# Finer interleaving of finishing work with a first convolution, and a later place for the strip copies

## The chip, the cores and the metric

One Trainium2 chip, one NeuronCore of it. The metric is device time in microseconds (us) of one execution; the kernel before has a median of 6257.3 us over 3 runs (6242.81 to 6264.0). Engines: PE is TensorE (matmuls and transposes), DVE is VectorE, ACT is ScalarE, POOL is GpSimd, SP is SyncE, which here only issues DMAs.

## The reference

For each of 16 samples x of 128 x 160 x 160, all in float32:

```
xp   = einsum('bchw,oc->bohw', x, proj_w)          # 128 -> 64 channels
att1 = route(xp,   depthwise 3x3 or 5x5)           # one kernel chosen per sample, by argmax of pooled logits
att2 = route(att1, depthwise 7x7, 9x9 or 11x11, dilation 3)
out  = concat([att1, att2])                        # 128 channels
a    = [mean over channels, max over channels] of out
gate = sum of the 2 channels of sigmoid(conv7x7(a) + sp_b)
result = out * gate + x
```

## The kernel before, in words

The program works on samples in turns. `samples` unrolls turns 0 to 3 and 15 to 17 and loops over 4 to 14. In turn s four samples are in work at once (`Turn`): sample s is projected and goes through the first convolution; sample k = s-1 goes through the second convolution; sample m = s-2 gets its gate and the second half of its output; sample n = s-3 gets the rest of the first half. All engines have their own hand-written order of work and meet by semaphores.

PE's turn has three stages, one behind the other:

- **Projection** (L947, L956 turns the result round): six blocks of rows of x. Behind fill 8 stands `turn_map2(m)` (L968), which turns the channel sums and maxima of sample m. DVE spreads them (`spread2`, L1326), SP stores them to `map2_d` (`store_map2`: L427 loads the other half, L436 stores) and loads both back (`load_maps`, L442). DVE's `combine` (L1332) waits for that, and only behind it come the last block's sums, the routing's small steps, and so the choice of weights that the first convolution needs. The 7x7 convolution of the maps is `spatial` (L1021).
- **First convolution** of sample s, 32 pairs of channels (`conv1`, L1011 and L1012). ACT widens and doubles each pair's band of weights and copies the result out (L823, L829, L834). Between the pairs stand pieces of *finishing* work that share the two banks psB: `turn_gate` ("gt", L1029); ten *f1* pieces (u = 6 to 15) of sample n, each 10 transposes (`finish1`, L1053) behind a product on DVE (`gate1`, L1397) and followed by DVE's two additions (L1406); and the five *f2* units of sample m, each 9 steps of 3 transposes (`finish2`, L1042), each step followed by DVE's additions into a tile xf (L1383). DVE multiplies L by the gate, one product per unit (`gate2`, L1364). A table `AFTER` says behind which group of two pairs which piece stands.
- **Second convolution** of sample k (L1074), 16 groups of 4 channels. POOL doubles its weights (L671), ACT brings the input (L854) and takes the result (L864). Behind groups 11 to 15 stand six *early* f1 pieces (u = 0 to 5) of sample m.

What the queues do around it: SP's turn is the maps and the gate; the loads of xf; then for each f2 unit `store_xf` (L457), `land` (L475, four DMAs that bring a sixth of the strips of sample k into the part of L that the unit has freed) and `load_xf` (L449) for the unit after next, which needs the tile that the store empties. Then `store_att1` (L485, 24 DMAs to `nat_d`), the first loads of the early pieces (L492 and L499), the load of one block of x (L489), `make_strips` (L535, 18 DMAs from `nat_d` to `strip_d`, DRAM to DRAM), and `early_pieces`, which per piece issues a load of att1 (L492), a store (L505) and a load of x (L499). POOL loads the other blocks of x (L634) and serves the f1 pieces of sample n (L682, L689, L695). ACT's `bring` of the first group waits until all six lands of the turn are through.

Semaphore order that matters: an f2 step writes bank t % 2 and waits for the additions of step t-2; an f1 piece waits for all f2 additions so far, and f2 work behind an f1 piece waits for that piece's additions.

## Time and profile before

| what | value |
|---|---|
| median of 3 runs | 6257.3 us |
| the profiled execution | 6248.61 us, span 6246.9 us |
| busy PE / DVE / ACT / POOL | 78% / 50% / 45% / 16% |
| mean granted TensorE clock | 0.873 |
| DMA, mean over the span | 206 GB/s |

The span is the time from the first to the last instruction; 1.7 us lie around it. Busy shares overlap between engines. The granted clock is a share of full speed, 2.4 GHz; 0.50 is the lower level, 1.2 GHz. A DMA share of 1 means that the core's 16 DMA engines were busy throughout.

### The profile page before, as it was taken

To read this page: it belongs to the slowest core of one execution; us is meant where nothing else is said; L and a number is where in the kernel's file an instruction comes from. 1 tells how busy PE (TensorE), PEld (TensorE's weight loads), DVE (VectorE), ACT (ScalarE), POOL (GpSimd) and SP (SyncE) were. 2 spreads that over 40 slices of the span, in tenths; PEclk is the share of its full clock that TensorE was granted. 3 is DMA by queue.
4 is the path that set the end of the run, shared out by engine and by line. 5 is a ranking of instruction groups with operands and counts; after the bars stand their busy time and mean duration, and the time that the engine had idled before them with its cause. 6 is when DMAs were issued, how large, how long until landed. Compare 5 with 4: busy or idle time off the path is not lost.

```text
span 6246.9 us, 164652 instructions
## 1 busy us (share of the span) xinstructions
PE 4902.2 (78%) x62816; PEld 3305.9 (53%) x62816; DVE 3144.4 (50%) x3931; ACT 2831.7 (45%) x5378; POOL 1030.5 (16%) x1574
## 2 busy tenths in 40 slices
PE   5688888978888897888888887788888788785463
PEld 2236474645646465564646546464554646455352
DVE  3316356554545655464464546545454565545445
ACT  3465544544445454544545454454444445452120
POOL 2002011211112121111211111121111112111232
PEclk9899998988889998988989888898898889887675
DMA  9646677868788786878868687886869778687957
GB/s 230 204 116 211 163 217 196 219 199 221 220 213 228 194 215 200 222 229 210 228 186 216 202 214 219 214 228 180 225 206 228 221 199 220 197 209 185 220 136 194
DMA packets 1033287, 1285.69 MB, mean 206 GB/s; under 512 B 670749, under 2 KB 865736, under 8 KB 1001885
## 3 DMA queue, kind: packets, MB, share of 16 engines
q1 hardware_dynamic: 899468, 723.43, 47.9%
q0 software_dynamic: 64304, 410.01, 21.1%
q10 hardware_dynamic: 69026, 146.11, 8.6%
q8 instruction: 259, 4.24, 0.3%
q14 instruction: 230, 1.88, 0.1%
HBM read 950.16 MB, written 456.70 MB: 225 GB/s over the span
## 4 chain that ended last, share of the span: by engine, by line
PE 34%; DMA 23%; SPq 21%; issue 9%; DVE 8%; ACT 2%; ACTq 1%; POOL 1%; DVEq 0%; POOLq 0%
SPq L485 12%; PE psA L1011 9%; PE psA L1012 9%; DMA X<-nat_d 6%; DMA out_dram<-RX 6%; DMA RX<-in_x_dram 5%; PE psC L1074 4%; SPq L535 4%; PE psA L947 3%; PE psB L1042 3%; SPq L436 3%; PE psB L1021 2%; PE psB L1053 2%; DVE MM L1299 2%; PE psB L956 2%
## 5 line engine op out<-in xcount | busy, mean ns | idle before, releaser
L1074 PE MATMUL psC<-RX 61*60 61x120 f32 (+7 forms) x49152 | 1538.6, 273 | 327.9 <-issue 154.7
L1074 PEld LDWEIGHTS psC<-RX 61*60 61x60 f32 x49152 | 1462.0, 137 | 404.4 <-issue 398.3
L864 ACT ACTIVATE L<-psC 124x120 f32 (+4 forms) x2048 | 393.9, 284 | 1119.9 <-PE psC L1074 1084.6
L1011 PE MATMUL psA<-X,RX 128*128 128x240 f32 x1280 | 640.1, 589 | 126.0 <-ACT RX L829 125.0
L671 POOL COPY RX<-RX 64x720 f32<-64x720 f32 x512 | 416.4, 816 | 1828.5 <-DMA RX<-w_d 1825.2
L1042 PE MATMUL psB<-ident,L 124*128 124x124 f32 x2160 | 413.4, 334 | 323.8 <-DVE RX L1383 283.2
L834 ACT ACTIVATE X<-psA,bias 128x246 f32<-128x246 f32 x1024 | 636.9, 735 | 56.6 <-issue 30.5
L1299 DVE TENSOR_REDUCE MM<-L 124x135 f32<-124x2160 f32 (+1 forms) x192 | 535.3, 2843 | 243.9 <-ACT L L864 243.9
L1012 PE MATMUL psA<-X,RX 128*128 128x240 f32 x1280 | 632.4, 583 | 0.0
L1383 DVE TENSOR_TENSOR RX<-psB,RX 128x360 f32<-128x360 f32 (+7 forms) x1200 | 366.4, 352 | 475.2 <-DMA RX<-in_x_dram 247.3
L854 ACT ACTIVATE RX<-L 128x1080 f32 (+1 forms) x256 | 541.0, 2121 | 131.0 <-DMA L<-strip_d 131.0
L947 PE MATMUL psA<-RX,projt 128*64 128x512 f32 x1600 | 462.9, 662 | 138.5 <-DMA RX<-in_x_dram 50.1
L1275 DVE TENSOR_REDUCE MM<-X 128x246 f32<-128x15744 f32 x16 | 264.8, 16553 | 587.5 <-ACT X L834 587.5
L823 ACT ACTIVATE RX<-RX 32x640 f32<-32x640 f32 x320 | 234.1, 736 | 718.1 <-PE psA L1012 585.4
L1042 PEld LDWEIGHTS psB<-ident,L 124*128 124x128 f32 x2160 | 290.6, 172 | 471.3 <-issue 445.9
L787 ACT ACTIVATE RX<-psA 128x512 f32<-128x512 f32 x480 | 287.5, 599 | 443.8 <-PE psA L947 400.9
L956 PEld LDWEIGHTS psB<-ident,RX 128*128 128x128 f32 x1920 | 207.1, 144 | 455.1 <-ACT RX L787 268.0
L1011 PEld LDWEIGHTS psA<-X,RX 128*128 128x128 f32 x1280 | 267.0, 219 | 338.3 <-issue 314.8
L1397 DVE TENSOR_TENSOR X<-X,G 80x1280 f32<-80x1280 f32 x126 | 190.5, 1522 | 444.1 <-DMA X<-nat_d 434.9
L1012 PEld LDWEIGHTS psA<-X,RX 128*128 128x128 f32 x1280 | 284.0, 222 | 231.1 <-issue 212.7
L1011 PE MATMUL psA<-X,MM 128*128 128x240 f32 x768 | 383.7, 588 | 16.5 <-ACT MM L829 14.9
L1012 PE MATMUL psA<-X,MM 128*128 128x240 f32 x768 | 379.5, 583 | 0.0
(122 smaller groups left out, 4969.7 us busy)
## 6 DMA issues: line engine op xcount, KB each, us to landing
RX<-in_x_dram POOLq DMA_DIRECT2D x48, 2560.0 KB, 16.4
RX<-w_d ACTq DMA_DIRECT2D x512, 180.0 KB, 4.4
RX<-in_x_dram SPq DMA_DIRECT2D x128, 720.0 KB, 10.3
out_dram<-RX SPq DMA_DIRECT2D x128, 720.0 KB, 10.3
nat_d<-X SPq DMA_DIRECT2D x320, 280.0 KB
L<-strip_d SPq DMA_DIRECT2D x192, 405.0 KB, 12.4
strip_d<-nat_d SPq DMA_DIRECT2D x48, 1440.0 KB
RX<-nat_d POOLq DMA_DIRECT2D x130, 400.0 KB, 6.7
```

Source lines behind the costliest of these rows:

```text
L485: sp.dma_start(dst, X[32 * k:32 * k + n, b, t0:t0 + T1, :]).then_inc(att1_stored, 16)
L671: nc.gpsimd.tensor_copy(w2t[j][64:128, :, :], w2t[j][0:64, :, :]).then_inc(w2_doubled, 1)
L834: ins = nc.scalar.activation(X[:, :, :, c:c + 1].rearrange("p b t c -> p (b t c)"), psA[pair % 2][:, ch * N1:(ch + 1) * N1], ACT.Identity, ...
L854: nc.scalar.activation(binf[q].rearrange("p (c f n) -> p c f n", c=G, f=5), Lc[:, :, bass.ds(g * G, G)].rearrange("p (n f) c -> p c f n", ...
L864: ins = nc.scalar.activation(dst[:, 0:NU2 - par, 15 * r:15 * r + nq, par, :], src[:, par:BR:2, :, :], ACT.Identity)
L947: ins = nc.tensor.matmul(o, projt[:, :], xsb[b][:, :, w0:w0 + FW], start=True, stop=True)
L1011: nc.tensor.matmul(o[:, :, 0:T1], w[:, ch, 96:224], rhs, start=True, stop=False, skip_group_check=True)
L1012: ins = nc.tensor.matmul(o[:, :, 1:1 + T1], w[:, ch, 224:352], rhs, start=False, stop=True, skip_group_check=True)
L1042: ins = nc.tensor.transpose(psB[t % 2][:, 124 * f:124 * f + 124], L[0:124, slot * C2:slot * C2 + 128], ident[0:124, 0:124])
L1074: ins = nc.tensor.matmul(o[:, :, 0:kk, a:b], w2t[2 * q + p][rows, ch, z:z + PB], src[rows, 2 * p + ch, 0:nf, 3 * cg + dc:3 * cg + dc + kk, ...
L1299: nc.vector.tensor_reduce(dst[0:124, mm, :].rearrange("p (f b k) -> p f b k", f=9, k=3)[:, :, par:BR:2, :], src[:, :, 0:NU2 - par, :, par, ...
L1383: return nc.vector.tensor_tensor(d, view(psB[t % 2][rows, :], 64 * g0 + c0, sdims), d, ALU.add)
```

## The change

Three things are edited.

1. On SP, `make_strips(s)` is issued behind `early_pieces(m)` where it stood ahead of it.
2. The table is by pair of channels, no longer by group of two pairs, on PE and DVE. In turns with a first convolution the f1 pieces 6 to 15 stand behind pairs 0, 3, 6, ..., 27 and the gate's turn behind pair 3. (Before: behind pairs 1, 3, 7, 11, 15, 17, 19, 21, 23, 25 and 3.) Turn 17 has a table of its own, changed likewise.
3. The f2 work is cut into 23 chunks of two steps where it was five units of nine. They stand behind pairs 4 to 22, one a pair and two behind pairs 7, 11, 15 and 19. (Before: one unit behind each of pairs 5, 7, 9, 11 and 13.) A unit's gate product on DVE follows the ninth step of the unit two before it, now inside a chunk.

```diff
+STEPS2 = 9 * NU2
+AFTER = {pair: [] for pair in range(C2 // 2)}
+for _u, _pair in zip(range(EARLY, NU1), (0, 3, 6, 9, 12, 15, 18, 21, 24, 27)):
+    AFTER[_pair].append(("f1", _u))
+AFTER[3].insert(0, ("gt", 0))
+for _c in range((STEPS2 + 1) // 2):
+    AFTER[4 + _c - (_c + 1) // 5].append(("f2", _c))
...
                     if t.next:
                         load_x2(s + 1)
-                    make_strips(s)
                     if t.early:
                         early_pieces(m)
+                    make_strips(s)
...
-            def finish2(m, u):
-                wait_alone(pe, att2_gated, NU2 * m + u + 1)
-                for t9 in range(9):
-                    t = 9 * u + t9
+            def finish2(m, c):
+                for t in range(2 * c, min(2 * c + 2, STEPS2)):
+                    u, t9 = divmod(t, 9)
                     p, k = divmod(t9, 3)
+                    if t9 == 0:
+                        wait_alone(pe, att2_gated, NU2 * m + u + 1)
...
-                for g in range(NG):
+                for pair in range(C2 // 2):
                     if t.new:
-                        for pair in (2 * g, 2 * g + 1):
-                            conv1(s, pair)
-                    for what, u in t.after[g]:
+                        conv1(s, pair)
+                    for what, u in t.after[pair]:
                         if what == "f1" and t.one:
                             if t.two:
-                                wait_alone(pe, f2_add, 45 * m + 9 * halves)
+                                wait_alone(pe, f2_add, 45 * m + min(2 * halves, STEPS2))
...
                     ins.then_inc(f2_add, 1)
+                    if t9 == 8 and u < NU2 - 2:
+                        gate2(m, u + 2)
...
                                 finish2(m, u)
-                                if u < NU2 - 2:
-                                    gate2(m, u + 2)
```

How the order moves, at two places. On PE, turn 3, the first convolution: four matmuls of L1011 and L1012 are one pair of channels, L1042 (L1050 in the changed kernel) are the f2 transposes, L1053 (L1061) an f1 piece. Before:

```order
L1042 MATMUL psB<-ident,L 128x124 x27
L1011 MATMUL psA<-X,RX 128x6x40
L1012 MATMUL psA<-X,RX 128x6x40
L1011 MATMUL psA<-X,RX 128x6x40
L1012 MATMUL psA<-X,RX 128x6x40
L1011 MATMUL psA<-X,RX 128x6x40
L1012 MATMUL psA<-X,RX 128x6x40
L1011 MATMUL psA<-X,RX 128x6x40
L1012 MATMUL psA<-X,RX 128x6x40
L1042 MATMUL psB<-ident,L 128x124 x27
L1053 MATMUL psB<-ident,RX 128x80 x10
```

And now:

```order
L1050 MATMUL psB<-ident,L 128x124 x6
L1018 MATMUL psA<-X,RX 128x6x40
L1019 MATMUL psA<-X,RX 128x6x40
L1018 MATMUL psA<-X,RX 128x6x40
L1019 MATMUL psA<-X,RX 128x6x40
L1061 MATMUL psB<-ident,RX 128x80 x10
L1050 MATMUL psB<-ident,L 128x124 x6
L1018 MATMUL psA<-X,RX 128x6x40
L1019 MATMUL psA<-X,RX 128x6x40
L1018 MATMUL psA<-X,RX 128x6x40
L1019 MATMUL psA<-X,RX 128x6x40
L1050 MATMUL psB<-ident,L 128x124 x12
```

27 transposes in a row have become 6 behind each pair (12 behind every fourth), and an f1 piece now has f2 transposes directly behind it, which before had a pair of channels or more between.

On SP, turn 2, behind the first loads of the early pieces. Before, from the end of the strips (the last of their 18 rows):

```order
L535 DMA strip_d<-nat_d 5x960
L535 DMA strip_d<-nat_d 5x1600
L492 DMA X<-nat_d 80x2x640
L505 DMA out_dram<-X 64x800 x2
L492 DMA X<-nat_d 80x2x640
L505 DMA out_dram<-X 64x800 x2
L499 DMA X<-in_x_dram 64x800 x2
```

And now, from the load of x on, and from the last store:

```order
L496 DMA X<-in_x_dram 128x5120
L499 DMA X<-nat_d 80x2x640
L512 DMA out_dram<-X 64x800 x2
L499 DMA X<-nat_d 80x2x640
L512 DMA out_dram<-X 64x800 x2
```

```order
L512 DMA out_dram<-X 64x800 x4
L542 DMA strip_d<-nat_d 48x4x1920
L542 DMA strip_d<-nat_d 48x960
L542 DMA strip_d<-nat_d 48x1600
L542 DMA strip_d<-nat_d 6x4x1920
```

The 18 strip copies have gone from ahead of the third early load of att1 to behind the last early store, that is, to just ahead of the next turn's L427 and L436.

## Rows read from the trace of the kernel before

**Rows 1.** The page: the span; the chain that ended last, by line.

```profile
span 6246.9 us, 164652 instructions
...
SPq L485 12%; PE psA L1011 9%; PE psA L1012 9%; DMA X<-nat_d 6%; DMA out_dram<-RX 6%; DMA RX<-in_x_dram 5%; PE psC L1074 4%; SPq L535 4%; PE psA L947 3%; PE psB L1042 3%; SPq L436 3%; PE psB L1021 2%; PE psB L1053 2%; DVE MM L1299 2%; PE psB L956 2%
```

**Rows 2.** Windows: us, busy PE, PEld, DVE, ACT, POOL (instructions), clock, DMA share, GB/s.

```profile
2276.00:2400.50 124.50, 104.34 (x3113) 98.95 (x3114) 77.65 (x33) 53.09 (x139) 24.25 (x30) 0.87 0.89 256
2407.10:2481.80 74.70, 63.56 (x294) 27.23 (x294) 47.38 (x86) 39.69 (x68) 10.57 (x17) 0.91 0.46 145
2481.80:2644.30 162.50, 138.88 (x500) 81.12 (x501) 67.72 (x122) 83.63 (x127) 25.98 (x46) 0.90 0.88 213
482.20:587.60 105.40, 91.77 (x3074) 88.02 (x3076) 67.26 (x21) 52.95 (x139) 22.66 (x30) 0.95 0.82 247
```

**Rows 3.** Timeline of PE: start, us, what, [idle before, releaser]; first convolution, turn 7.

```profile
2481.83 1.14 PE L1011 MATMUL psA<-X,RX 128*128 128x240 f32 x2 [6.44 <-ACT RX L829]
...
2488.45 0.87 PE L1053 MATMUL psB<-ident,RX 80*128 80x80 f32 x10
...
2506.55 0.83 PE L1042 MATMUL psB<-ident,L 124*128 124x124 f32 x6 [0.42 <-DVE RX L1406]
...
2556.48 5.57 PE L1042 MATMUL psB<-ident,L 124*128 124x124 f32 x21 [8.16 <-DVE RX L1383]
```

**Rows 4.** Groups of instructions in that stage (xcount | busy us, mean ns | idle before).

```profile
L1042 PE MATMUL psB<-ident,L 124*128 124x124 f32 x135 | 24.7, 321 | 15.6 <-DVE RX L1383 14.6 <-DVE RX L1406 0.4
...
L1383 DVE TENSOR_TENSOR RX<-psB,RX 128x360 f32<-128x360 f32 (+7 forms) x75 | 22.8, 352 | 29.2 <-DMA RX<-in_x_dram 14.5 <-PE psB L1042 14.1
L1364 DVE TENSOR_TENSOR L<-L,G2s 124x3456 f32<-124x3456 f32 x5 | 18.7, 3751 | 0.0
```

**Rows 5.** Timeline of SP's issues in the same stage.

```profile
2526.06 12.59 SPq L475 DMA_DIRECT2D L<-strip_d  x4
2540.60 2.26 SPq L449 DMA_DIRECT2D RX<-in_x_dram  x2
...
2576.75 25.06 SPq L475 DMA_DIRECT2D L<-strip_d  x8
```

**Rows 6.** The page: DMA issues, KB each, us to landing.

```profile
L<-strip_d SPq DMA_DIRECT2D x192, 405.0 KB, 12.4
```

**Rows 7.** Timeline of PE in the second convolution of turn 6.

```profile
2354.12 4.27 PE L1074 MATMUL psC<-RX 61*60 61x135 f32 x96 [4.09 <-POOL RX L671]
...
2384.98 1.60 PE L1053 MATMUL psB<-ident,X 80*128 80x80 f32 x10 [4.54 <-DVE X L1406]
```

**Rows 8.** Timeline of SP's issues there, and in the projection behind it.

```profile
2341.19 19.12 SPq L535 DMA_DIRECT2D strip_d<-nat_d  x18
...
2402.96 6.05 SPq L505 DMA_DIRECT2D out_dram<-X  x4
...
2428.32 19.10 SPq L436 DMA_DIRECT2D map_d<-RX  x12
```

**Rows 9.** The chain of waits, in order of time, over the same stretch.

```profile
2360.67 22.14 DMA X<-nat_d
...
2389.02 4.17 DMA X<-nat_d
...
2453.60 3.71 DMA minc<-map_d
```

**Rows 10.** Windows of 20 us: the first two of the projection of turn 7.

```profile
2406.00:2426.00 20.00, 18.77 (x89) 7.69 (x89) 14.58 (x21) 11.18 (x19) 3.16 (x6) 0.85 0.14 36
2426.00:2446.00 20.00, 19.64 (x99) 7.55 (x100) 16.37 (x19) 12.92 (x23) 2.30 (x3) 1.00 0.79 283
```

**Rows 11.** Timeline of DVE: combine, in the same projection.

```profile
2457.33 0.83 DVE L1332 TENSOR_TENSOR minc<-RX,minc 48x640 f32<-48x640 f32 x1 [9.95 <-DMA minc<-map_d]
```

**Rows 12.** Timeline of PE in turn 16, which has no first convolution.

```profile
5839.99 1.47 PE L1042 MATMUL psB<-ident,L 124*128 124x124 f32 x6 [1.27 <-DVE X L1406]
...
5867.57 1.57 PE L1053 MATMUL psB<-ident,X 80*128 80x80 f32 x10 [11.23 <-DVE X L1406]
```

More of the change, by code:

```diff
@@ L61 @@
 EARLY = 6
-AFTER = {0: (("f1", 6),), 1: (("gt", 0), ("f1", 7)), 2: (("f2", 0),), 3: (("f2", 1), ("f1", 8)),
-         4: (("f2", 2),), 5: (("f2", 3), ("f1", 9)), 6: (("f2", 4),), 7: (("f1", 10),), 8: (("f1", 11),),
-         9: (("f1", 12),), 10: (("f1", 13),), 11: (("f1", 14),), 12: (("f1", 15),), 13: (), 14: (), 15: ()}
-AFTER_LAST = {0: (("gt", 0), ("f1", 0), ("f2", 0)), 1: (("f1", 1), ("f1", 2), ("f2", 1)), 2: (("f1", 3), ("f1", 4), ("f2", 2)),
-              3: (("f1", 5), ("f1", 6), ("f2", 3)), 4: (("f1", 7), ("f1", 8), ("f2", 4))}
-AFTER_LAST.update({g: (("f1", g + 4),) for g in range(5, 12)})
-AFTER_LAST.update({g: () for g in range(12, 16)})
+STEPS2 = 9 * NU2
[5 more added lines that the diff above has]
+    AFTER[4 + _c - (_c + 1) // 5].append(("f2", _c))
+AFTER_LAST = {pair: [] for pair in range(C2 // 2)}
+AFTER_LAST[0] = [("gt", 0), ("f1", 0)]
+for _c in range((STEPS2 + 1) // 2):
+    AFTER_LAST[1 + _c].append(("f2", _c))
+for _u in range(1, NU1):
+    AFTER_LAST[2 * _u].append(("f1", _u))
 def conv_block(nc, x, proj_w, w1, b1, w2, b2, att1_w, att1_b, att2_w, att2_b, sp_w, sp_b, out):
@@ L1365, in gate2, with finish2 @@
                                         ALU.mult).then_inc(att2_gated, 1)
-            def finish2(m, u):
-                q = u % 2
-                rows = slice(0, 128 if u < 4 else 64)
-                dve.wait_ge(xf_loaded[q], xf_count(m, u))
-                for t9 in range(9):
-                    t = 9 * u + t9
+            def finish2(m, c):
+                for t in range(2 * c, min(2 * c + 2, STEPS2)):
+                    u, t9 = divmod(t, 9)
+                    q = u % 2
+                    rows = slice(0, 128 if u < 4 else 64)
                     p, k = divmod(t9, 3)
+                    if t9 == 0:
+                        dve.wait_ge(xf_loaded[q], xf_count(m, u))
                     dve.wait_ge(f2_mm, 45 * m + t + 1)
@@ L1427, in turn @@
                         gate1(n, u)
-                for g in range(NG):
-                    for what, u in t.after[g]:
+                for pair in range(C2 // 2):
+                    for what, u in t.after[pair]:
                         if what == "f1" and t.one:
```

## The prediction

> **What bounds the kernel now.** I read the page first. No engine is full, and the chain that ended last changes hands all the time: SP's issues, transfers, PE [rows 1]. So the question is not how busy an engine is but what ends each stage of a turn. I therefore cut one steady turn by PE's stages [rows 2]: second convolution 124.5 us (2276.0 to 2400.5, turn 6), then turn 7's projection and routing 74.7 us (from 2407.1), its first convolution with all finishing work 162.5 us up to the next stage's start. With the 6.6 us between the first two that is 368.3 us a turn. The DMA engines are at 0.89 and 0.88 in the two convolutions and at 0.46 in the projection. The fourth window is the second convolution of turn 1, which has no early pieces: 105.4 us.
>
> In the first convolution the timeline of PE [rows 3] shows two pairs of channels in 6.6 us (2481.83 to 2488.45), so 3.3 us each; an f1 piece in 0.87 us; two f2 steps, where nothing holds them, in 0.83 us. It also shows one idle time of 8.16 us before f2 transposes. The groups [rows 4] give the sum: 15.6 us idle before f2 transposes, nearly all put down to DVE's additions, which themselves waited 14.5 us for the load of xf and 14.1 us for PE. In the second convolution PE waits 4.09 us for doubled weights and 4.54 us for DVE [rows 7]. At that time SP's strips are in flight: 18 issues in 19.12 us from 2341.19 [rows 8], and the early load of att1 that is issued right behind them takes 22.14 us to land where a later one takes 4.17 us [rows 9]. In the projection DVE waits 9.95 us for the maps of sample m [rows 11].
>
> **The change, part by part.** Fourteen turns (2 to 15) have both convolutions and the gate work; I price one and multiply. The sum is made against the profiled execution, 6248.61 us, which is 8.7 us under the median of the runs.
>
> *Strips behind the early pieces: second convolution.* The third load of att1 is then issued before 2360.67, with the strips gone from its queue, and lands in 4.2 us rather than 22.1 [rows 9]: the 4.54 us before the f1 piece goes. The 4.09 us for weights (POOL waits for their DMA) goes too, since only one block of x and small loads are left beside them. That is 8.6 us. PE's clock is 0.87 over this stage against 0.95 in turn 1 [rows 2], where PE idled less; the stretch behind each of the two stalls runs nearer the lower level, 1.2 GHz. A cross-check from above: turn 1 ran the same 3072 matmuls in 105.4 us although its strips were in flight; six early pieces at 0.87 us make it 110.6. I take 112, a gain of 12.5 us. Bounds: 6 (only half of the 8.6 was the strips', and some clock) and 17 (the 13.9 of the cross-check and 3 for what turn 1's own strips cost).
>
> *The same strips: next projection.* The last early store is issued at 2409.0 [rows 8]; behind it SP issues hardly anything until its map stores at 2428.32, and the strips' 19.1 us of issue fit almost exactly. So those stores start about 1 us late. The transfers fit less well. The DMA share is 0.14 in the first 20 us of the projection and 0.79 in the next 20 [rows 10], when two blocks of x and the maps move. The strips fill the first window, and some 4 us of them spill into the second. Behind that stands a chain with no slack: map stores, then the load of minc (lands in 3.71 us, [rows 9]), then `combine`, which already waits 9.95 us [rows 11] and holds the routing and so the first convolution. I take 4.5 us lost. Bounds: 0 (all fits) and 18 (what the strips cost the load behind them, 22.1 less 4.2).
>
> *Finer interleaving: first convolution.* PE's own work does not change: 32 pairs at 3.3 (106), 45 steps at 0.41 (18.7), ten f1 pieces at 0.87 (8.7), the gate's turn 0.7: 134 us. Of the 162.5 us, 28.5 are waits, some 4 of them at the end, where ACT brings the next stage's input; these stay. What goes: the wait of every second f2 step for the additions two steps back, since a pair of channels now stands between two chunks, and part of the waits for xf. What comes:
> - Six f1 pieces now have an f2 chunk directly behind, which waits for the piece's additions. Turn 16 shows that wait, 1.27 us [rows 12]; at full clock I take 1.0: 6 us.
> - The first f2 chunk stands one pair behind an f1 piece, while DVE is still at two gate products of 3.75 us each [rows 4]: 4 us.
> - The other gate products now fall inside the chunks. Where a double chunk follows at once (pairs 11 and 15) PE waits for the additions behind the product: 1 and 5 us.
> - xf: unit u+2's tile needs the store of unit u, then come 12.59 us of `land` on SP, then the load's issue at 2540.60 [rows 5] and its transfer; PE goes on at 2556.48 [rows 3], 30 us behind the start of that `land` at 2526.06. A unit and its two pairs took little over 10 us before (3.7 and 6.6), so the load was late. Now a unit stands over 3.6 pairs (11.9) with its 3.7, an f1 piece or two and the waits above, up to 20 us; two units take up to 40, more than the 30. I leave 3 us.
> - ACT, which needs nearly a pair's time for its four steps, 1 us.
>
> 134, 20 and 4 are 158 us against 162.5: 4.5 us gained, far less than the 15.6 us of idle time suggest. Bounds: 3 us lost and 12 gained (all waits but the 6 and the 6 for the gate gone).
>
> *What is late next.* The last eight lands were issued from 2576.75 [rows 5] of a stage that began at 2481.8, 95 us in; they will be from about 120 us in (23 of 32 pairs, all f2 steps, eight f1 pieces and the 20 us). They take 25.06 us of issue, and the last one lands 12.4 us behind its issue [rows 6]; `bring` needs that, and takes the stage's last 4 us. 120 and 37 are 157, against 154, where `bring` could begin; with the DMA less crowded at the stage's end, as I expect with fewer f1 pieces there, a few us less. I add nothing, and keep 5 us as a bound.
>
> *The ends.* In turn 16 the f1 pieces at the end wait up to 11.23 us each for their loads [rows 12]; five stood in a row, now two, the others lie in the waits of f2. Turn 17 likewise has its f1 work spread more evenly. I take 15 us off for both, between 0 and 30.
>
> *Sum.* A turn: 12.5 and 4.5 gained, 4.5 lost, 12.5 net. Fourteen turns: 175. With the ends 190. 6248.6 less 190 is 6059, which I round to 6060 us. The offset to the median is inside the uncertainty and is left out.
>
> **A rule against the change.** The second window of the projection shows x and the strips' spill at one place [rows 10]. The Trainium skill, in "DMA: Bandwidth & Descriptors", section "Issuing engines are not separate DMA queues", says that transfers issued by SP, ACT and POOL run on the same 16 DMA engines and interleave. By that rule putting the strips elsewhere on SP takes no traffic away, and POOL's loads of x feel them although they are on another queue. If all 18 us of the upper bound came back in the projection, the sum of a turn would be 1 us lost and not 12.5 gained; that mechanism is the last rival below. What speaks against its full size is the trace's own 0.14.
>
> **The rivals.**
> - *Both gains come in full.* With 0.88 of DMA in the first convolution spread more evenly, loads land sooner and xf is never late: 12 there, 14 in the second, 3 lost in the projection. 23 times 14 and 20 for the ends: 5907 us. For it: the waits for transfers shrink with density. Against: the waits from the gate products stay.
> - *The f2 work ends too late.* The first convolution gains nothing, and the lands hold the second for 5 us. 12.5 less 4.5 less 5 is 3 a turn, 42, and the ends 15: 6192 us. For it: there is no margin in the 157 us above.
> - *The strips were not what stalled the second convolution.* The block of x issued just ahead of them was. The stage gains 6 us, the others as in the forecast: 6 a turn, 84, and the ends 15: 6150 us. Against: the 22.14 us.
> - *Slower: the strips hold the maps.* SP's map stores queue behind strips that have not drained, and blocks of x slow them further. The 18 us of the upper bound, and 7 us in which SP itself is held at issue (four lands took 12.59 us, 3.1 each, where a strip copy takes 1.1 [rows 5, 8]): 25 us in the chain that has no slack. 25 less 17 is 8 lost a turn, 112, less the 15: 6346 us. It decides from about 18 us on. Against: 17 us of near idle DMA in front.
>
> **How the numbers follow.** Forecast 0.42; both gains in full 0.20; f2 too late 0.17; not the strips 0.12; slower 0.09. The predicted time is 6060 us. The range, 5905 to 6225 us, takes in all but the slower rival and a part of the largest gain. A measurement of this kernel tells about 0.3% (19 us) from no change. Faster by more than that: 0.42, 0.20, 0.12 and nearly all of 0.17, together 0.87. Within: 0.04, from the edge of the second rival. Slower: 0.09.
>
> **What would show it.** Second convolution about 112 us, no idle time over 2 us before the early pieces' L1061, and their loads of att1 landing in 4 to 6 us. Projection and routing 79 us, with DVE waiting about 14 us for minc. First convolution 154 us, the idle time before f2 transposes spread over many waits of about 1 us behind f1 pieces and one of 4 to 5 us each behind the gate's turn and at pair 15. A new wait of ACT's `bring` for strips would prove the second rival. A projection over 92 us would prove the last.

## The result, and the profile after

The change made the kernel faster: **6081.5 us** in the median (6060.95 to 6094.04, 4 runs) beside 6258.6 us for the kernel before in the same rounds (4 runs), a ratio of 0.9726 with a 95% interval of 0.9700 to 0.9753. 6060 us had been predicted, in a range of 5905 to 6225. The profiled execution took 6060.95 us with a span of 6059.5 us, so 187.4 us less span than before [rows 1].

The page after: the span; the chain that ended last, by engine and by line; groups (busy us, mean ns | idle before); DMA issues with us to landing.

```profile
span 6059.5 us, 164966 instructions
...
PE 46%; DMA 24%; issue 9%; DVE 8%; SPq 8%; ACT 3%; ACTq 1%; POOL 1%; DVEq 0%; POOLq 0%; another core or an unknown queue 0%
PE psC L1082 16%; PE psA L1018 10%; PE psA L1019 9%; DMA RX<-in_x_dram 7%; DMA RX<-w_d 5%; SPq L443 3%; DMA out_dram<-RX 3%; PE psB L1050 3%; PE psA L954 2%; PE psB L1028 2%; DMA RX<-nat_d 2%; DMA X<-nat_d 2%; DVE MM L1306 2%; PE psB L1061 2%; SPq L492 2%
...
L1082 PE MATMUL psC<-RX 61*60 61x120 f32 (+7 forms) x49152 | 1486.0, 268 | 285.4 <-POOL RX L678 103.8
...
RX<-in_x_dram POOLq DMA_DIRECT2D x48, 2560.0 KB, 19.5
...
L<-strip_d SPq DMA_DIRECT2D x192, 405.0 KB, 10.5
```

The chain by line reads, for SP, L443 3% and L492 2%: the stores of att1, which held 12% of it before (L485, now L492), are down to 2%, the strips with their 4% (L535) have left its head, and the map stores (L436, now L443) keep their 3% [rows 1]. The second convolution's matmuls (L1082, then L1074) take 1486.0 us with 285.4 us idle before them; before it was 1538.6 and 327.9. POOL's loads of x land in 19.5 us where they took 16.4.

The windows of the same turn as in [rows 2, 10]: second convolution of turn 6; projection and routing, then first convolution, of turn 7; second convolution of turn 1; the first 20 us of that projection, the next 20, and 20 more. Columns as there.

```profile
2212.90:2322.50 109.60, 96.19 (x3113) 91.56 (x3114) 79.27 (x33) 53.20 (x139) 25.43 (x30) 0.94 0.89 234
2329.20:2405.70 76.50, 63.30 (x294) 26.29 (x294) 44.76 (x82) 39.59 (x68) 10.57 (x17) 0.92 0.68 224
2405.70:2567.30 161.60, 134.73 (x500) 81.16 (x500) 66.86 (x122) 82.63 (x127) 26.05 (x46) 0.90 0.89 214
478.80:582.80 104.00, 91.38 (x3074) 87.61 (x3074) 67.31 (x21) 53.01 (x139) 22.57 (x30) 0.95 0.82 250
2329.20:2349.20 20.00, 19.86 (x98) 8.00 (x98) 13.25 (x24) 11.08 (x19) 3.50 (x6) 0.92 0.98 319
2349.20:2369.20 20.00, 16.87 (x80) 6.54 (x80) 12.69 (x12) 11.21 (x20) 0.52 (x1) 0.91 0.80 314
2369.20:2389.20 20.00, 17.40 (x80) 6.40 (x78) 9.81 (x12) 11.54 (x20) 1.45 (x2) 0.91 0.34 108
```

The second convolution is 14.9 us shorter (124.5 to 109.6). In this turn PE's busy time gives 8.2 of that (104.34 to 96.19, with the granted clock up from 0.87 to 0.94), its idle time 6.7. The projection is 1.8 us longer, the first convolution 0.9 us shorter. One turn is a small sample, so the same cut was made at every turn. This table has the means, from the first matmul of a stage to that of the next, each row from one profiled execution; turn 2 has no f1 piece in its first convolution and stands apart, and "turn 16" runs from the start of turn 15's second convolution to the end of turn 16. e3 is left out, because its profiled execution was a slow one of 8120.13 us, where its four others took 6015.74 to 6054.02.

```
                                   first conv  second conv  projection,  first conv  turn 16  turn 17
                                   turns 3-15  turns 2-14   turns 3-15   of turn 2
before                               164.3       130.7        73.2        155.8      427.1    222.0
the change                           162.9       115.6        76.8        141.3      433.8    212.0
e1 strips only                       164.5       116.5        75.9        157.7      435.5    220.0
e2 table only                        164.1       131.2        72.0        141.6      430.9    215.7
e4 tiny strips                       163.3       116.0        71.8        140.9      422.9    217.6
e5 gates later                       162.0       115.3        76.2        141.6      430.7    216.9
e6 strips after maps                 163.4       115.8        75.4        140.5      432.1    217.7
e7 gates later, f1 alone             161.5       115.8        76.8        140.0      434.5    211.5
e8 gates later, strips after maps    163.5       115.5        75.3        140.3      432.9    216.4
e9 load first                        162.6       116.4        76.2        139.0      428.4    215.7
e10 load first, gates later          159.3       116.0        76.5        140.2      427.9    215.4
e11 tiny lands, gates later          150.6       116.2        77.1        140.7      410.9    216.9
e12 e10, strips after maps           159.9       115.5        75.2        138.6      429.2    217.0
```

Summed over the program, the change gives: second convolution 13 times 15.1, 197 us; first convolution 13 times 1.5 and 14.5 in turn 2, 34 us; projection 13 times 3.6 and 3.5 in turn 2 lost, 51 us; turn 15's second convolution and turns 16 and 17 together 3 us; the first two turns 5 us. Added up before rounding, that is the 187.4 us.

**Second convolution.** PE's timeline in turn 6 (start, us, what, [idle before, releaser]), at the places of [rows 7], and the chain at that of [rows 9]:

```profile
2288.36 4.22 PE L1082 MATMUL psC<-RX 61*60 61x135 f32 x96 [3.17 <-POOL RX L678]
...
2302.26 0.91 PE L1061 MATMUL psB<-ident,X 80*128 80x80 f32 x10
```

```profile
2307.18 5.83 DMA X<-nat_d
...
2344.18 15.15 DMA RX<-in_x_dram
```

No early piece waits any more (0.32 us is left before the sixth). The third load of att1, the one that took 22.14 us behind the strips, is now issued at 2287.49 and lands in 9.0 us; the row of 5.83 us above is the fifth. Over turns 3 to 14 the third takes 11.2 us in the mean, where it took 22.4. But the wait for doubled weights stayed: 3.17 us against 4.09 here, and all waits for them together are 7.6 us a turn in the mean, against 6.8 before.

Turn 6 doesn't stand for all turns in how the gain is made up. The same windows over the 13 turns 2 to 14, up to the next projection, give a mean busy time of PE of 103.2 us before and 98.3 after, and idle time of 27.5 and 17.3. So of the 15.1 us gained, 4.9 are shorter work at a higher clock (0.88 to 0.94) and 10.2 are waits: some 6.6 of them before the early pieces, and some 4.4 that the trace puts down to no releaser.

**Projection.** SP's issues around its start, and DVE's waits in it:

```profile
2324.21 4.12 SPq L512 DMA_DIRECT2D out_dram<-X  x4
2328.66 15.88 SPq L542 DMA_DIRECT2D strip_d<-nat_d  x18
...
2352.50 20.75 SPq L443 DMA_DIRECT2D map_d<-RX  x12
2379.02 0.82 SPq L449 DMA_DIRECT2D minc<-map_d  x2
```

```profile
2359.36 0.25 DVE L1205 TENSOR_REDUCE part<-RX 128x2 f32<-128x56 f32 x1 [4.50 <-DMA RX<-in_x_dram]
...
2382.06 0.82 DVE L1339 TENSOR_TENSOR minc<-RX,minc 48x640 f32<-48x640 f32 x1 [9.63 <-DMA minc<-map_d]
```

The map stores begin 23.3 us behind the stage's start (2352.50 less 2329.2), before 21.2 us (2428.32 less 2407.1, [rows 2, 8]), and combine's wait did not grow: 9.63 us against 9.95 [rows 11]. DVE's waits for blocks of x did, 4.50 us where before it was 1.70; the chain above shows that block in flight for 15.15 us. They don't set the stage's length, though, since DVE waits 9.63 us for the maps behind them. What sets it is the chain of the maps: their stores hold SP for 20.75 us and not 19.10, the load of minc is issued 49.8 us into the stage and not 46.5 (2379.02 and 2453.60 [rows 9]), and combine begins 52.9 us in and not 50.2 (2382.06 and 2457.33). In the mean of turns 3 to 15 combine begins at 54.0 and not at 49.5 us, and in e4 below, without the strips' bytes, at 47.9. So the maps come 4.5 us later and the stage is 3.6 us longer; DVE's own wait for minc is only 9.7 us against 8.9, because DVE comes to it later as well.

**First convolution.** Its groups in turn 7, to set against [rows 4], and single waits from PE's timeline:

```profile
L1391 DVE TENSOR_TENSOR RX<-psB,RX 128x360 f32<-128x360 f32 (+7 forms) x75 | 22.4, 349 | 36.1 <-PE psB L1050 33.6 <-DMA RX<-in_x_dram 2.3
L1050 PE MATMUL psB<-ident,L 124*128 124x124 f32 x135 | 22.3, 302 | 17.4 <-DVE RX L1416 11.0 <-DVE RX L1391 6.3
...
L1061 PE MATMUL psB<-ident,RX 80*128 80x80 f32 x100 | 9.6, 248 | 4.8 <-DVE RX L1391 3.3 <-DVE G2s L1364 1.5
```

```profile
2431.56 1.48 PE L1050 MATMUL psB<-ident,L 124*128 124x124 f32 x6 [4.31 <-DVE RX L1416]
...
2441.98 0.82 PE L1050 MATMUL psB<-ident,L 124*128 124x124 f32 x6 [1.14 <-DVE RX L1416]
...
2475.08 1.08 PE L1061 MATMUL psB<-ident,RX 80*128 80x80 f32 x10 [3.29 <-DVE RX L1391]
...
2497.80 0.85 PE L1050 MATMUL psB<-ident,L 124*128 124x124 f32 x3 [3.60 <-DVE RX L1391]
```

DVE's wait for xf fell from 14.5 to 2.3 us, as the finer table should bring about. PE's idle time in the stage nevertheless rose, from 23.6 (162.5 less 138.88) to 26.9 us (161.6 less 134.73): the 4.31 us behind the two gate products, 1.14 us behind each f1 piece, and two waits of 3 to 4 us at the later products.

**Turn 16.** PE's timeline from turn 15's second convolution to that of turn 16, after and then before, and SP's issues there, after and before:

```profile
5413.71 12.94 PE L1082 MATMUL psC<-RX 61*60 61x135 f32 x384 [3.71 <-ACT RX L861]
...
5524.11 2.65 PE L975 MATMUL psC<-ident,MM 124*27 124x124 f32 x12 [13.08 <-DVE MM L1314]
...
5557.88 9.46 PE L1028 MATMUL psB<-minc,wsp 112*104 112x320 f32 x28 [28.74 <-DVE minc L1342]
...
5720.04 7.82 PE L1082 MATMUL psC<-RX 61*60 61x135 f32 x192 [26.80 <-ACT RX L861]
```

```profile
5597.76 12.74 PE L1074 MATMUL psC<-RX 61*60 61x135 f32 x349 [3.86 <-ACT RX L854]
...
5717.22 2.65 PE L968 MATMUL psC<-ident,MM 124*27 124x124 f32 x12 [12.99 <-DVE MM L1307]
...
5740.77 10.69 PE L1021 MATMUL psB<-minc,wsp 112*104 112x320 f32 x28 [18.51 <-DVE minc L1335]
```

```profile
5515.34 12.89 SPq L542 DMA_DIRECT2D strip_d<-nat_d  x18
...
5530.05 21.06 SPq L443 DMA_DIRECT2D map_d<-RX  x12
...
5690.18 14.85 SPq L482 DMA_DIRECT2D L<-strip_d  x8
```

```profile
5722.79 10.75 SPq L436 DMA_DIRECT2D map_d<-RX  x12
...
5851.99 21.14 SPq L475 DMA_DIRECT2D L<-strip_d  x8
```

ACT's `bring` there, after and before:

```profile
5717.51 4.06 ACT L861 ACTIVATE RX<-L 128x1080 f32<-128x1080 f32 x2 [149.07 <-DMA L<-strip_d]
```

```profile
5883.51 3.95 ACT L854 ACTIVATE RX<-L 128x1080 f32<-128x1080 f32 x2 [130.97 <-DMA L<-strip_d]
```

Turn 15's second convolution, up to the transposes behind it, takes 110.4 us (5413.71 to 5524.11) where it took 119.5, so 9 us less. The block is 6.7 us longer all the same: turn 16 itself loses 16. It has no projection to hide the strips in, so there they do hold the maps: 28.74 us of waiting, not 18.51. The 26.80 us are ACT's `bring`, which waits for the last landing copies. These now come late: the last eight are issued 166 us behind the transposes and not 135, and `bring` begins at 193 and not 166 us. The strips' move is one part of that, the finer table the other, for it puts f1 pieces between the f2 chunks that stood behind them before. The single edits (e1 and e2 below) part the two. With the strips alone, PE waits 28.8 us for the maps, and the block takes 435.5 us. With the table alone it waits 18.1 us for them, but the last landing copies are issued at 157 us, and PE waits 27.8 us for `bring`: 430.9 us. Before, PE had f1 pieces and a wait of 10.2 us for weights in that time, so its second convolution begins only 12 us later now, not 27.

### The profile page after: what moved, and what is told of

Read it like the earlier page. It is cut to its first block, busy times and chain, and to the rows that moved or that the text cites. A ratio compares the mean times of both kernels' runs of the same rounds, so it can differ in the third digit from the quotient of the medians.

```text
span 6059.5 us, 164966 instructions
## 1 busy us (share of the span) xinstructions
PE 4793.2 (79%) x62816; PEld 3248.4 (54%) x62816; DVE 3141.7 (52%) x3931; ACT 2822.0 (47%) x5378; POOL 1042.6 (17%) x1574
## 4 chain that ended last, share of the span: by engine, by line
PE 46%; DMA 24%; issue 9%; DVE 8%; SPq 8%; ACT 3%; ACTq 1%; POOL 1%; DVEq 0%; POOLq 0%; another core or an unknown queue 0%
PE psC L1082 16%; PE psA L1018 10%; PE psA L1019 9%; DMA RX<-in_x_dram 7%; DMA RX<-w_d 5%; SPq L443 3%; DMA out_dram<-RX 3%; PE psB L1050 3%; PE psA L954 2%; PE psB L1028 2%; DMA RX<-nat_d 2%; DMA X<-nat_d 2%; DVE MM L1306 2%; PE psB L1061 2%; SPq L492 2%
## 5 line engine op out<-in xcount | busy, mean ns | idle before, releaser
L1082 PE MATMUL psC<-RX 61*60 61x120 f32 (+7 forms) x49152 | 1486.0, 268 | 285.4 <-POOL RX L678 103.8
L1082 PEld LDWEIGHTS psC<-RX 61*60 61x60 f32 x49152 | 1413.4, 134 | 357.7 <-issue 349.3
L1050 PE MATMUL psB<-ident,L 124*128 124x124 f32 x2160 | 384.8, 320 | 325.8 <-DVE RX L1391 151.1
L1050 PEld LDWEIGHTS psB<-ident,L 124*128 124x128 f32 x2160 | 298.2, 168 | 461.0 <-issue 451.6
L1416 DVE TENSOR_TENSOR RX<-psB,RX 128x400 f32<-128x400 f32 x260 | 138.8, 570 | 504.1 <-PE psB L1061 502.3
L1018 PE MATMUL psA<-X,MM 128*128 128x240 f32 x768 | 382.1, 586 | 14.0 <-ACT MM L836 11.2
## 6 DMA issues: line engine op xcount, KB each, us to landing
RX<-in_x_dram POOLq DMA_DIRECT2D x48, 2560.0 KB, 19.5
```

What stands on the lines that cost most here:

```text
L1018: nc.tensor.matmul(o[:, :, 0:T1], w[:, ch, 96:224], rhs, start=True, stop=False, skip_group_check=True)
L1050: ins = nc.tensor.transpose(psB[t % 2][:, 124 * f:124 * f + 124], L[0:124, slot * C2:slot * C2 + 128], ident[0:124, 0:124])
L1082: ins = nc.tensor.matmul(o[:, :, 0:kk, a:b], w2t[2 * q + p][rows, ch, z:z + PB], src[rows, 2 * p + ch, 0:nf, 3 * cg + dc:3 * cg + dc + kk, ...
```

## The experiments

All times are medians beside runs of the kernel before on the same chip; the ratio is to those. One theory was held from the start (the two edits are independent, the strips win in the second convolution and lose in the projection); what holds the first convolution was open, and the theory on it changed twice.

**e1 and e2: each edit alone.** e1 moves `make_strips(s)` behind `early_pieces(m)` in the kernel before; e2 moves it back in the changed kernel.

```
-                    make_strips(s)
                     if t.early:
                         early_pieces(m)
+                    make_strips(s)
```

> The kernel before with one edit: the strip copies issued behind the early pieces. Theory (the two edits are separate, and this one carries nearly all the gain): second convolution 110 us a turn where it was 124.5, projection and routing 77 where it was 73, first convolution unchanged at 164; 14 turns of -11 us, so about 6100 us. Rival (the strips' move pays only together with the finer table, since dense f2 work still crowds the queues): less than half of that, 6170 us or more.

> The changed kernel with the strip copies back ahead of the early pieces, so the finer table alone. Theory: the first convolution loses 1 to 2 us in turns 3 to 15 and 14 us in turn 2, the second convolution stays at 124 us, so 6215 to 6235 us. Rival (the table gives the second convolution room too, by a better state of the queues at its start): second convolution under 118 us and a time under 6180 us.

Measured: e1 6117.45 us, 0.9798 (0.9780 to 0.9816); e2 6216.55 us, 0.9949 (0.9930 to 0.9968). Both came out on the side of the theory. The product, 0.9748, is within the interval of the whole change, so the edits add. Windows of e1 (second convolution of turn 6, first of turn 7), then of e2 (the same):

```profile
2235.90:2345.50 109.60, 96.68 (x3113) 92.02 (x3114) 78.93 (x33) 53.00 (x139) 24.53 (x30) 0.94 0.89 232
2430.70:2595.30 164.60, 139.80 (x500) 81.88 (x500) 67.69 (x122) 83.59 (x127) 26.05 (x46) 0.88 0.88 211
```

```profile
2256.20:2380.50 124.30, 100.67 (x3113) 95.47 (x3113) 77.25 (x33) 52.89 (x139) 22.94 (x30) 0.87 0.90 256
2459.00:2623.30 164.30, 134.81 (x500) 80.55 (x501) 66.86 (x122) 82.61 (x127) 26.03 (x47) 0.90 0.88 211
```

The strips alone make the second convolution 109.6 us at a clock of 0.94; the table alone leaves it at 124.3 us and 0.87. The whole gain there, clock included, is the strips'. The table wins 14.2 us in turn 2 and in the full turns nothing (164.1 against 164.3): PE's busy time falls from 138.88 to 134.81, and its idle time grows by about as much. In turn 2, which has no f1 piece for a chunk to wait behind, the change shortens both: the work from 131.1 to 125.0 us and the idle time from 21.0 to 12.5.

**e3 and e4: what the strips' bytes cost.** Before, and in the changed kernel, each strip copy from turn 2 on is cut to 16 numbers a row: as many copies and rows, a small part of the bytes. The rest of the strips holds old values.

```
+                            run = cut or run
                             mid = [[54 * 1920, strips]] if strips > 1 else []
```

> The kernel before, but from turn 2 on each strip copy moves 16 numbers a row instead of 960 to 1920: the copies of turns 2 to 15 are left out but for their issue. Theory (the strips' data, not their issue on SP, stalls the second convolution): 110 us there with the strips in their old place, projection 73, so about 6045 us. Rival (the block of x issued just ahead, or SP's 19 us of issue, stalls it): 118 us or more there, 6150 us or more.

> The changed kernel with the same cut: the strip copies of turns 2 to 15 left out but for their issue. Theory (the 3.6 us that the projection lost are the strips' data beside the blocks of x and the maps): projection and routing back at 73 us, second convolution at 110, so about 6030 us. Rival (they are SP's issue time ahead of the map stores): projection stays at 76 to 77 us, 6070 us or more.

Measured: e3 6042.56 us, 0.9664 (0.9632 to 0.9696); e4 5996.49 us, 0.9595 (0.9574 to 0.9615). Of e3 only the time is known, not its stages. It is the 6045 us of the theory: the strips' data cost the kernel before some 200 us, not their issue on SP, which e3 keeps. The first 40 us of e4's projection of turn 7, in windows of 20:

```profile
2308.00:2328.00 20.00, 19.86 (x96) 8.33 (x98) 15.29 (x26) 11.18 (x19) 3.50 (x6) 0.88 0.23 52
2328.00:2348.00 20.00, 19.48 (x99) 7.39 (x96) 16.09 (x15) 13.87 (x24) 1.96 (x2) 1.00 0.77 278
```

Without the bytes the second window is back at 19.48 us of PE work (16.87 in the change), and the projection at 71.8 us. The 18 copies still hold SP for 14.84 us of issue (15.88 in the change), so all the 5.0 us that separate the change from that are transfers, not issues. POOL's loads of x land in 15.6 us in e4 and 16.2 in e2, in 18.7 in e1 and 19.5 in the change. Turn 16 falls from 433.8 to 422.9 us, and PE's wait for the maps in it from 28.7 to 18.4: the strips' bytes hold the maps there. The second convolution stays (116.0 against 115.6): once they are behind it, the strips cost it nothing.

**e5: the gate products out of the way.** The finer table left PE waiting behind DVE's products. Here a product is only noted as owed, and DVE does it behind its next f2 chunk.

```
                     if t9 == 8 and u < NU2 - 2:
-                        gate2(m, u + 2)
+                        owed.append(u + 2)
```

> The changed kernel with DVE's gate products moved: the second one of a turn behind the first f2 chunk, and those for units 2 to 4 behind all f2 additions of their pair of channels, not inside a chunk. Theory (the first convolution gained little because waits for DVE's in-order gate products took the place of the old ones): the wait before the first f2 chunk falls from 4.3 us to under 1, the waits of 2.7 and 3.3 us at pair 15 go; the stage falls from 163 to about 154 us, so 1.9% faster than the changed kernel, 0.955 of the kernel before. Rival (the stage is held by transfers, at a DMA share of 0.88, and a wait removed comes back before the next load): stage 160 us or more, 0.968 or more.

Measured: 6053.12 us, 0.9693 (0.9665 to 0.9720). The theory fell, and the rival's 160 us or more and 0.968 or more came: the first convolution takes 162.0 us, 0.9 less than in the change. The group of DVE's f2 additions in turn 7:

```profile
L1391 DVE TENSOR_TENSOR RX<-psB,RX 128x360 f32<-128x360 f32 (+7 forms) x75 | 22.4, 349 | 39.5 <-PE psB L1050 24.1 <-DMA RX<-in_x_dram 15.0
```

The waits behind the gates went, and a wait for xf of 15.0 us stands in their place, as large as the 14.5 us before the change. The load of xf had been just hidden by the other waits. In the mean of turns 3 to 15 DVE waits for xf 16.5 us before, 2.7 in the change and 15.1 in e5.

**e6, e7 and e8: strips behind the map loads, and an f1 piece never beside a chunk.** e6 moves the strips once more, behind `load_maps`; e7 is e5 with a table in which no f2 chunk stands right behind an f1 piece; e8 is e5 and e6 together.

```
                     load_maps(m)
+                    if t.conv2:
+                        make_strips(t.k)
                     load_gate(m)
```

```
+for _c, _pair in enumerate((4, 5, 5, 7, 7, 8, 10, 10, 11, 11, 13, 14, 14, 16, 16, 17, 19, 19, 20, 20, 22, 23, 23)):
+    AFTER[_pair].append(("f2", _c))
```

> The changed kernel with the strip copies issued later still: in the next turn, behind the load of the maps and ahead of the gate's. Theory (the projection loses 4 to 5 us only because the strips' data meet blocks of x and the maps): projection and routing fall from 77 to 73 us, the first convolution rises by 1 us at most, 0.964 of the kernel before. Rival (strips cost the same wherever they fall, since all transfers share the DMA engines): projection 73 us but first convolution 167 us or more, 0.973 again.

> As e5_gates_later, and no f2 chunk stands behind the same pair as one of the f1 pieces 8 to 15: the 23 chunks stand behind pairs 4 to 23, two behind nine of them where it was four. Theory (each f1 piece with a chunk directly behind costs PE 1.1 us, each double chunk 0.6 us): six waits of 1.1 us go and five of 0.6 come, the stage falls 3 us more, 0.6% under e5_gates_later. Rival (DVE's additions are as late for the next pair's work, or ACT, which needs nearly the pair's time, takes the slack): no difference beyond 0.2%.

> The edits of e5_gates_later and e6_strips_after_maps together. Theory (one works in the first convolution, the other in the projection, and they add up): 0.946 of the kernel before, about 5920 us. Rival (both push transfers into the first convolution, which is near the DMA's limit): 0.953 or more, and PE or DVE waiting for xf or for the strips' landing there.

Measured: e6 6062.06 us, 0.9700 (0.9673 to 0.9726); e7 6053.58 us, 0.9690 (0.9664 to 0.9717); e8 6053.65 us, 0.9681 (0.9653 to 0.9710). e6 wins 1.4 us a turn in the projection, not the theory's 4, and loses 0.5 in the next stage, less than the rival's 4; its ratio can't be told from the change's. Combine does begin 6.5 us sooner than in the change (47.5 us in, means), but the strips are now in flight when ACT loads the first convolution's weights: from the end of the routing to the first pair 10.9 us pass and not 7.5. In turn 7 ACT waits 5.55 us for the band (L833). And DVE waits for the gate's loads behind the strips:

```profile
L1357 DVE COPY RX<-RX 27x120 f32<-27x120 f32 x9 | 1.5, 230 | 6.9 <-DMA RX<-gate_d 6.9
```

e8's two halves do not add up to the theory's 0.946: its first convolution takes 163.5 us, and its time is e5's. e7 does not differ from e5, as its rival said: its mean wait for xf is 21.5 us a turn, so what was taken from the f1 waits came back there. Two edits aimed at PE's and DVE's waits had now moved them to the same load. Two explanations were left: the order on SP (store of unit u, four landing copies, load of unit u+2), or the bytes that the DMA engines move in this stage at a share of 0.9.

**e9, e10 and e11: order against bytes.** e9 is the change, and e10 is e5, with the load ahead of the landing copies:

```
                         store_xf(m, u)
-                        if t.conv2:
-                            land(s - 1, u)
                         if u < 3:
                             wait_alone(sp, out2_stored[u % 2], xf_count(m, u))
                             load_xf(m, u + 2)
+                        if t.conv2:
+                            land(s - 1, u)
```

e11 is e5 with the landing copies of turns 3 and on (its expectation says 4, but the edit spares only turns below 3), those issued between the stores of xf, cut to 16 numbers a row (L keeps old values in the rest):

```
-                            land(s - 1, u)
+                            land(s - 1, u, None if isinstance(s, int) and s < 3 else 16)
```

> The change with one thing else: while f2 runs, the SyncE queue issues the two loads of x2 (load_xf(u + 2)) before the four landing copies land(u), no longer after them. Theory: the first convolution is held by the cycle of a row block of x2 on that queue (store, four landing copies of 7 to 9 us of issue, load, landing), so that what was won on TensorE was given back as waits for x2; with the landings behind the load this cycle is 8 us shorter three times a turn. In this kernel VectorE waits only 2.7 us a turn for x2, so it wins little by itself: the first convolution 162.9 -> 160 to 162, about 6040 us, ratio 0.966. Rival: the stage is held by what the DMA engines move (their share in it is 0.91), the landings then come later by as much as the loads come earlier and something else waits (ScalarE for the landed strips, VectorE for the parts of the sum in the next stage): 162 to 164 us, ratio 0.970 to 0.976.

> e5_gates_later with the loads of x2 ahead of the landing copies. There VectorE waited 15.1 us a turn for x2, the first convolution took 162.0 us and the run had a ratio of 0.9693. Theory (the cycle of the row block through the landings holds it): that wait falls to under 6 us, the first convolution to 152 to 156 us, some 90 to 120 us in all, ratio 0.950 to 0.956. Rival (what the DMA engines move holds it): the wait moves once more, the first convolution stays at 160 to 163 us, ratio 0.966 to 0.972.

> e5_gates_later with the landing copies of the turns 4 and on that are issued while f2 runs cut to 16 numbers a row (as many copies, a fraction of the bytes; the strips L then hold old values). The bytes of the landings are thereby out of the first convolution while their issue time on SyncE stays. If the DMA engines' bytes hold the stage: their share falls from 0.90, the wait of VectorE for x2 falls from 15.1 us to under 5 and the first convolution to 150 to 156 us, ratio 0.945 to 0.957. If it is the order on the SyncE queue that holds it, through issue time and the stores' landing: the wait stays at 10 us or more, the stage at 159 us or more, ratio over 0.962.

Measured: e9 6060.90 us, 0.9708 (0.9683 to 0.9733), with 162.6 us in the first convolution, on the side of its rival; e10 6014.11 us, 0.9637 (0.9613 to 0.9661); e11 5897.08 us, 0.9445 (0.9424 to 0.9466). The same group and the stage in e10, then in e11:

```profile
L1391 DVE TENSOR_TENSOR RX<-psB,RX 128x360 f32<-128x360 f32 (+7 forms) x75 | 22.3, 348 | 38.4 <-PE psB L1050 23.4 <-DMA RX<-in_x_dram 14.7
```

```profile
L1391 DVE TENSOR_TENSOR RX<-psB,RX 128x360 f32<-128x360 f32 (+7 forms) x75 | 22.3, 349 | 28.0 <-PE psB L1050 26.0 <-DMA RX<-in_x_dram 1.7
```

```profile
2359.60:2510.40 150.80, 133.73 (x503) 80.21 (x504) 66.62 (x122) 82.96 (x127) 26.07 (x46) 0.92 0.81 193
```

Taking the landings' bytes out, with every copy still issued (four of them hold SP for 6.9 to 7.4 us, in e5 for 7.4 to 8.7), ends the wait for xf (1.7 us) and brings the stage from 162.0 to 150.6 us. Changing the order alone (e10 against e5) brings 2.7 us of that 11.4 (159.3), less than the theory's 6 or more and a little more than the rival's 2 at most. SP's issues in e10 show why the order helps so little:

```profile
2427.01 8.56 SPq L482 DMA_DIRECT2D L<-strip_d  x4
2435.77 4.66 SPq L464 DMA_DIRECT2D out_dram<-RX  x2
2455.07 1.22 SPq L456 DMA_DIRECT2D RX<-in_x_dram  x2
```

The load no longer stands behind the landing copies, but the next store does: from its issue at 2435.77 to the load that waits for its end 19.3 us pass, 12.4 at the same place in the change (2467.81 to 2480.20). So the landings lengthen the cycle of xf from whichever side they stand on. In e11 both the copies' transfers and what queues behind them are gone; which of the two counts more can't be told apart by these runs, and stays open.

**e12: all that helped.** e10 with the strips behind the map loads (the edits of e5, e6 and e9 together).

> e10 with the strip copies behind the maps too (as in e8). e8 had a ratio of 0.9681, with 5.6 to 7 us a turn more of waiting for the gate and 15.9 us for x2 in the first convolution. Theory: with the cycle of x2 shorter, the saving of 1.5 us a turn in the projection stays: ratio 0.947 to 0.955, the fastest of all. Rival: the first convolution is held by the bytes, 162 to 164 us, ratio 0.966 to 0.972, no better than e8.

Measured: 6003.46 us, 0.9621 (0.9587 to 0.9654). It is between the theory's 0.947 to 0.955 and the rival's 0.966 to 0.972, with 159.9 us in the first convolution and 75.2 in the projection. It is the fastest kernel that leaves no work out, by about 1% against the change (0.9726), but its interval overlaps that of e10, so the strips' second move adds nothing that can be told.

## Why the prediction was right, and where only its sum was

The median was 21 us above the 6060 predicted, and each stage of a full turn moved to the side foreseen. The sum was made for the profiled execution: 190 us less, and 187.4 were measured. But so close an agreement is luck, errors that cancel: against the terms of the sum, the second convolution gave 31 us more (206 with turn 15's, not 175), the first 29 less (34, not 63), the projection cost 12 less (51, not 63), the ends lost 6 where they were to give 15, and the first two turns gave 5 that were not in the sum.

- **Second convolution: 12.5 us forecast, 15.1 measured** (13 turns). Right in its mechanism: no early piece waits, and e1 and e2 put all of the gain on the strips, which is also the end of the third rival, for in e1 the block of x still stands ahead. The working was wrong inside. "The 4.09 us for weights goes too" failed: 3.17 us of it stayed, and over all turns this wait did not shrink (6.8 us a turn before, 7.6 after). What holds the weights is open. The third load of att1 was to land in 4.2 us and took 9.0. The sum came near because more went elsewhere, before the early pieces and in idle time that no wait explains: 10.2 us of idle time in the mean against its 8.6, and 4.9 us by the clock against its 3.9. Turn 6 alone would say otherwise (6.7 and 8.2). The cross-check by turn 1, 13.9 us, was the better guide.
- **Projection: 4.5 us lost forecast, 3.6 measured.** The spill was right in size and in cause (e4 returns it with the bytes alone, 71.8 us), and so was the chain behind it: the stores of the maps start 2.1 us later where 1 was said, and combine begins 4.5 us later in the mean (54.0 and 49.5 us in). Only the sign was badly chosen. DVE's wait for minc did not go from 10 to 14 us, because DVE comes to it later as well, behind blocks of x that land in 19.5 us and not 16.4. The rule of the Trainium skill in "DMA: Bandwidth & Descriptors", section "Issuing engines are not separate DMA queues", is borne out as a mechanism, for POOL's loads of x felt SP's strips (15.6 us to land in e4, which lacks their bytes, and 19.5 with them); by the full 18 us of its rival the stage would be 91 us, and it is 76.8.
- **First convolution: 4.5 us forecast, 1.5 measured** in the full turns, and 14.5 in turn 2, which has no f1 pieces and was priced like the others. The list of new waits was good: 10 us for additions behind f1 pieces and the first gate products (11.0 in the rows), 9 for the later products and xf (9.6). The step that failed is "PE's own work does not change, 134 us". It took 45 f2 steps at the best reading, 0.41 us, 18.7 in all, while the group's own row said 24.7 and the stage's window 138.88 us of busy time [rows 2, 4]. So the kernel before had 139 us of work and 24 of waits, not 134 and 28.5; there was less to win. After, the work is indeed 134.7 us, so it did change, and the waits are 26.9, more than before and more than the 24 of the sum. (Its list of signs has 154 us for this stage where its sum has 158; 161.6 came.)
- **xf, of which 3 us were left, was only just covered.** The prediction reckoned its cycle at 30 us against 40 of cover, and in the change DVE does wait only 2.3 us. e5 and e7 show that the cover was the other waits: take them away and DVE waits 15 to 21 us for it. e11 shows that the landings' bytes stand behind it. This is also why the first rival, both gains in full, did not come about: the better orders tried here won 3.6 us of the stage at most (e10).
- **Ends: 15 us gained forecast, 6 lost measured.** Turn 17 gave 10 us (the kernels e2, e4, e6 and e9, with the same table, show 4 to 6 in theirs), turn 16 lost 16: the slower rival, strips that hold the maps, is real in the one turn with no projection to hide them in (28.74 us against 18.51), and so is the second, f2 work that ends too late (last landing copies at 166 us and not 135, 26.80 us of waiting for `bring`). The forecast costed both in the full turns only.
- **f2 ends too late: in the full turns it did not.** The last landing copies are issued 127 us into the stage (2532.73 less 2405.70), 120 had been said, but they take 12.02 us and not 25.06, and the second convolution begins without a new wait.

## What to carry to other kernels

When a wait goes, look for the transfer that it covered: what two edits took from PE's and DVE's waits here came back as the same load. A new order of issue won 2.7 us of the stage, fewer bytes beside that load 11.4. Take an engine's own work in a stage from its busy time in the window, not from the best single reading times a count. And price a moved burst of copies in the odd turns as well, since a turn without the stage that hides it pays in full. Read a split into work and waits over all turns, too: one turn had it the wrong way round.

## What the runs showed of the hardware

- How long SP is held at issue varies twofold for the same copies: the 12 map stores took 10.75 us in turn 16 before, 19.10 with blocks of x beside them [rows 8], and 20.75 and 21.06 behind the strips. The DMA share does not order them: it was 0.91, 0.77, 0.68 and 0.77 in these four stretches. The last eight landing copies took 25.06 us of issue before and 12.02 after, at shares of 1.08 and 1.02. What it is in the traffic beside them that counts, no run here shows.
- With stalls gone the granted clock rose too: in the second convolution from 0.88 to 0.94 in the mean of 13 turns, and PE's busy time for the same matmuls fell from 103.2 to 98.3 us, half of the 10.2 us of idle time that went. Single turns scatter: in turn 6 it fell by 8.2 us and the idle time by 6.7.
- The strips, hidden behind PE work, cost nothing where the engines had been at 0.14: with a DMA share of 0.98 PE was busy for 19.86 of those 20 us. The price came in the next 20 us, at 0.80.
